# A recommender tower on one core: the end after the last interaction layer is computed in another order

## The chip, the cores and the metric

One Trainium2 chip, one of its cores. The metric is the device time of one launch in microseconds (us). The kernel before took 900.58 us, the median of 3 runs (899.3 to 905.62).

## The reference, cut to what matters

For each of 512 samples, 32 table rows of 32 numbers are looked up. Two interaction layers (CIN) follow, each of 128 maps, and three dense layers:

```
e   = gathered rows                              # (512, 32, 32): sample, field h, position d
c0  = relu(sum over h, m of  e[h] * e[m]  * filter_0[h, m, n])      # (512, 128, 32)
c1  = relu(sum over h, m of  e[h] * c0[m] * filter_1[h, m, n])      # (512, 128, 32)
z   = concat(sum over d of c0, sum over d of c1)                    # (512, 256)
h   = concat(z, dense_ctx)                                          # (512, 272), dense_ctx is (512, 16)
h   = maximum(h @ W_top1 + b_top1, 0)                               # (512, 512)
h   = maximum(h @ W_top2 + b_top2, 0)                               # (512, 256)
y   = h @ W_top3                                                    # (512, 1)
```

All of it is float32. The kernel calls the sum over d of c0 `h0`, and the sum over d of c1 `h1`.

## The kernel before, in words

**Tiles.** A tile is 4 samples by 32 positions, 128 rows. There are 128 tiles, in 32 groups of four; a group is 512 columns wide. `over_groups` (L91) writes groups 0, 1, 29, 30 and 31 out one by one and loops over those between. `u` is the tile in its group, 0 to 3.

**Products in two halves.** Most products split an operand into a rounded part in the format fp32r (`_hi`) and the remainder, whole minus rounded part (`_lo`). They compute hi*hi, hi*lo and lo*hi, three TensorE instructions of 512 columns (L637, L638, L643 for the second interaction layer). A product of two plain float32 tiles, such as L693, is one call that the trace shows as two MATMUL instructions.

**The second interaction layer** is nearly all of the time. Each tile has eight banks of 512 columns, `k` = 0 to 7. TensorE (PE) computes a bank in one of six PSUM buffers in turn (RING). ScalarE (ACT) takes banks 0, 1, 3, 5, 6 out with the scale by the embedding (L399, four instructions of 128 columns to a bank), and VectorE (DVE) takes banks 2, 4, 7 (L523). A bank can be written anew once the one six before it has been taken out. GpSimd (POOL) adds two quarters of a tile's products once banks 0 to 3 are out (`fold`, L330). DVE then sums the rest in two halves (`reduce`, L537), and takes the maximum with zero (`rectify`, L544), which signals `c1_ready`. PE sums over d by a product of 4 columns (`sum_h1`, L648), three tiles later.

**Orders.** Each engine runs its own instructions in the order in which they are written. DVE's order in a tile is: bank 2, second half of `reduce` of two tiles before, bank 4, `rectify` of two tiles before, first half of `reduce` of the tile before, bank 7. In the last group (31) no interaction of a further group is prepared, and there DVE also rounds the weights of the top layers (`round_top`, L565, L569) in tiles 1 and 2, and POOL computes their remainders (L358) after the folds of tiles 2 and 3.

**The end.** After the last bank, PE runs `sum_h1` of tile 1, then for each of four blocks `j` of 128 outputs the float32 products with h0 (L693) and with the 16 dense columns (L694), both in plain float32. It then runs `sum_h1` of tiles 2 and 3. ACT copies `h1` rounded out of PSUM in two pieces (L439: 504 columns early, the last 8 late), DVE forms its remainder (L602), and PE runs 12 products of 512 columns with h1 (L701, L702, L705). ACT then reads each block of the first dense layer twice, rounded and whole, both with the bias (L443, L444); DVE subtracts (L605). PE runs 24 products of the second dense layer (L710, L711, L714), ACT rectifies twice (L447), PE runs the last product (L720), ACT copies it (L449), and SP writes it out (L282).

**Queues.** SP issues all other transfers, among them seven for the top layers (L268 to L274) behind those of group 2. POOL issues the gathers.

## Time and profile before

| | |
|---|---|
| median of 3 runs | 900.58 us |
| profiled execution: time | 904.71 us |
| profiled execution: span of the core | 902.9 us |
| PE busy | 879.3 us, 97% |
| DVE busy | 780.5 us, 86% |
| ACT busy | 782.9 us, 87% |
| POOL busy | 750.6 us, 83% |
| granted clock, mean over the span | 0.989 |
| transfers in the first of 40 slices of the span | 179 GB/s |

Times in the rows further down are us from the start of the span. A busy time of PE counts matmuls whose ends are modelled, and neighbours overlap; the distance from start to start is what one costs. The granted clock is given as a share of full speed: 1.00 is 2.4 GHz and 0.50 is 1.2 GHz.

### The profile page before, as it was taken

Reading aid. Unit: us, or ns where it says so; the run is one execution under the profiler, and the core shown is the slowest. Engines: PE = TensorE matmul, PEld = TensorE weight load, DVE = VectorE, ACT = ScalarE, POOL = GpSimd, SP = SyncE. Lnnn points to the kernel's source line nnn. Section 1 sums busy time; section 2 is a strip of 40 time slices with the busy share of each in tenths; the row PEclk is TensorE's granted clock in tenths of the full one; section 3 lists DMA queues with packets and bytes.
Section 4 is the critical chain, followed back from the end, with each engine's and each line's share of the span. In section 5 each row is a group of like instructions: output and inputs, shape, how many; then the busy total and the mean of one; then the engine's idle time right before and its main releaser. Section 6 shows DMA issues by size and latency. Waiting matters only on the chain.

```text
span 902.9 us, 17442 instructions
## 1 busy us (share of the span) xinstructions
PE 879.3 (97%) x3758; PEld 689.7 (76%) x3758; DVE 780.5 (86%) x903; ACT 782.9 (87%) x2744; POOL 750.6 (83%) x542
## 2 busy tenths in 40 slices
PE   3899999999999999999999999999999999999988
PEld 2678877777887777788777778877777887777844
DVE  4588888999888899988889998888989888898991
ACT  2699899999989999999989999989999999999942
POOL 5599889898888989888898988889899898988430
PEclk9999999999999999999999999999999999999987
DMA  5432222221222222122222212222221122220000
GB/s 179 127 115 79 80 74 78 78 64 34 67 78 73 77 78 68 33 64 78 73 77 78 68 35 61 78 73 77 78 75 33 56 78 73 77 78 1 1 1 0
DMA packets 42810, 60.85 MB, mean 67 GB/s; under 512 B 6274, under 2 KB 17154, under 8 KB 42787
## 3 DMA queue, kind: packets, MB, share of 16 engines
q1 hardware_dynamic: 38690, 58.48, 21.1%
q0 software_dynamic: 4096, 2.11, 1.6%
q8 instruction: 9, 0.15, 0.1%
q14 instruction: 15, 0.11, 0.0%
HBM read 56.37 MB, written 4.20 MB: 67 GB/s over the span
## 4 chain that ended last, share of the span: by engine, by line
PE 95%; DMA 1%; ACT 1%; DVE 1%; issue 1%; POOL 0%; SPq 0%; DVEq 0%; ACTq 0%; POOLq 0%
PE ps_y L637 27%; PE ps_y L643 26%; PE ps_y L638 26%; PE ps_c L616 6%; PE ps_h L648 2%; PE ps_c L625 2%; PE ps_c L624 2%; PE ps_c L626 2%; PE ps_c L622 1%; ACT prod L399 1%; PE ps_y L694 1%; PE ps_y L693 1%; DMA second<-et_scratch 1%; DMA gat<-table,rows_now 0%; POOL gat L292 0%
## 5 line engine op out<-in xcount | busy, mean ns | idle before, releaser
L399 ACT ACTIVATE prod<-ps_y,es 128x128 f32<-128x128 f32 x2560 | 715.7, 434 | 72.7 <-PE ps_y L643 68.7
L537 DVE TENSOR_REDUCE csum<-prod 128x64 f32<-128x1536 f32 x256 | 447.3, 1748 | 10.4
L637 PE MATMUL ps_y<-w_hi,c_hi 128*128 128x512 f32 x1024 | 437.3, 427 | 2.1 <-ACT prod L399 1.3
L643 PE MATMUL ps_y<-w_hi,c_lo 128*128 128x512 f32 x1024 | 400.9, 392 | 0.0
L638 PE MATMUL ps_y<-w_lo,c_hi 128*128 128x512 f32 x1024 | 400.4, 391 | 0.0
L330 POOL TENSOR_TENSOR prod<-prod 128x1024 f32<-128x1024 f32 x128 | 308.3, 2408 | 55.6 <-ACT prod L399 48.8
L523 DVE TENSOR_TENSOR prod<-ps_y,es 128x512 f32<-128x512 f32 x384 | 256.8, 682 | 76.2 <-PE ps_y L643 72.8
L637 PEld LDWEIGHTS ps_y<-w_hi,c_hi 128*128 128x128 f32 x1024 | 192.8, 188 | 54.7 <-issue 18.2
L638 PEld LDWEIGHTS ps_y<-w_lo,c_hi 128*128 128x128 f32 x1024 | 192.9, 188 | 50.2 <-issue 14.9
L643 PEld LDWEIGHTS ps_y<-w_hi,c_lo 128*128 128x128 f32 x1024 | 192.1, 188 | 43.4
L321 POOL TENSOR_TENSOR z<-first,second 128x512 f32<-128x512 f32 x155 | 198.6, 1299 | 9.1 <-DMA second<-et_scratch 9.1
L292 POOL DMA_INDIRECT gat<-table,rows_now x128 | 124.8, 975 | 52.9 <-POOL rows_now L303 26.2
L311 POOL TENSOR_TENSOR z_lo<-z,z_hi 128x512 fp32r<-128x512 f32 x93 | 118.9, 1296 | 0.0
L616 PE MATMUL ps_c<-z,w_sum 128*128 128x512 f32 x128 | 65.3, 591 | 0.7 <-DVE z L492 0.7
L368 ACT ACTIVATE z_hi<-z 128x512 fp32r<-128x512 f32 x64 | 51.3, 801 | 12.0 <-DVE z L492 11.1
L648 PEld LDWEIGHTS ps_h<-ones_b,c 128*128 128x128 f32 x256 | 48.2, 190 | 13.0 <-issue 1.5
L544 DVE TENSOR_REDUCE c<-csum 128x128 f32<-128x256 f32 x128 | 52.1, 407 | 0.1
L648 PE MATMUL ps_h<-ones_b,c 128*128 128x4 f32 x256 | 36.3, 213 | 0.8 <-DVE c L544 0.8
L616 PEld LDWEIGHTS ps_c<-z,w_sum 128*128 128x128 f32 x128 | 23.9, 188 | 6.4 <-DVE z L492 1.5
L624 PE MATMUL ps_c<-z_hi,w_hi 128*128 128x512 f32 x64 | 25.8, 403 | 1.5 <-DVE z_lo L557 1.5
L625 PE MATMUL ps_c<-z_hi,w_lo 128*128 128x512 f32 x64 | 26.2, 409 | 0.0
L626 PE MATMUL ps_c<-z_lo,w_hi 128*128 128x512 f32 x64 | 26.0, 406 | 0.0
(65 smaller groups left out, 278.0 us busy)
## 6 DMA issues: line engine op xcount, KB each, us to landing
second<-et_scratch SPq DMA_DIRECT2D x160, 256.0 KB, 4.4
first<-et_scratch SPq DMA_DIRECT2D x32, 256.0 KB, 3.3
et_scratch<-gat SPq DMA_DIRECT2D x64, 64.0 KB
prod<-w SPq DMA_DIRECT2D x4, 512.0 KB, 7.1
gat<-table,rows_now POOLq DMA_INDIRECT x128, 2.4
wt_sb<-wt SPq DMA_DIRECT2D x2, 512.0 KB
prod<-w0a SPq DMA_DIRECT2D x1, 320.0 KB, 3.0
prod<-w0b SPq DMA_DIRECT2D x1, 320.0 KB, 3.3
```

What stands on the lines that cost most here:

```text
L292: pool.indirect_dma_start(out=gat[:, g.r, u * D:(u + 1) * D], out_offset=None, in_=table, in_offset=bass.IndirectOffsetOnAxis(ap=rows_now[ ...
L311: nc.gpsimd.tensor_tensor(z_lo[:, k, :], z[:, k, :], z_hi[:, k, :].bitcast(F32), ALU.subtract).then_inc(z_lo_ready, 1)
L321: nc.gpsimd.tensor_tensor(z[:, k, :], first[:, :], second[:, k, :], ALU.mult).then_inc(z_ready, 1)
L330: nc.gpsimd.tensor_tensor(high, high, low, ALU.add).then_inc(folded, 1)
L399: last = nc.scalar.activation(prod[:, buffer_of(g, u), h // 2, :, h % 2], ps_y[:, bank_of(g, u, k), j * N:(j + 1) * N], ACT.Copy, scale=es ...
L523: nc.vector.tensor_tensor(prod[:, buffer_of(g, u), pairs, :, :], ps_y[:, bank_of(g, u, k), :].rearrange("p (a n t) -> p a n t", n=N, t=2), ...
L537: nc.vector.tensor_reduce(csum[:, maps, 0], prod[:, buffer_of(g, u), FOLD // 2:F // 2, maps, :].rearrange("p a n t -> p n a t"), AX.XY, AL ...
L616: nc.tensor.matmul(ps_c[:, :], w0_sum[:, k, :], z[:, k, :].rearrange("p (b u d) -> p u b d", u=TG, b=BT), start=(k == 0), stop=False)
L637: nc.tensor.matmul(out, hi, w_hi, start=True, stop=False)
L638: nc.tensor.matmul(out, hi, w_lo, start=False, stop=False)
L643: nc.tensor.matmul(out, lo, w_hi, start=False, stop=True).then_inc(y_ready, 1)
L648: nc.tensor.matmul(ps_h1[:, bass.ds(g.times(TG * BT, u * BT), BT)], c1[:, u % 2, :], ones_b[:, :], start=True, stop=True).then_inc(h1_done, 1)
```

## The change

It concerns the last group and what comes after it.

- The dense columns are stacked with the bias. The host builds an operand of 81 rows: three copies of the 16 dense columns at rows 0, 32 and 64, and a row of ones behind the first and the third; for the weights the bias stands in these rows. On the chip both operands are rounded. In rows 32 to 47 of the values and rows 64 to 80 of the weights the remainder takes the place of the rounded part (`stack_rest`). One product then gives hi*hi, lo*hi and hi*lo, with the bias in it.
- h0 is split into `h0_hi` and `h0_lo`, and its part of the first layer is three fp32r products for each block in place of one in float32.
- The products with h1 are divided by columns: the first 504 (`early`) come before `sum_h1` of the last two tiles, the last 8 (`late`) behind it. ACT copies the early columns twice, and POOL forms the early remainder; DVE forms the late one.
- Ten products whose result nobody reads (KEEP_WARM) stand before `sum_h1` of the last two tiles.
- The roundings of the weights are on ACT (five `round_top`), and POOL has three remainders, of wt2, of both halves of wt1, and of h0.
- ACT reads each block of the first dense layer once. DVE takes the remainder from PSUM, as max(x, 0) minus the rounded part.
- SP issues six transfers for the top layers; the two for the dense columns have 81 rows in place of 16.

```diff
 B, F, D, N, DENSE = 512, 32, 32, 128, 16
 TOP1, TOP2 = 512, 256
+STACK = 64 + DENSE + 1
...
+        dense_x_sb = sb("dense_x_sb", [STACK, B])
+        dense_w_sb = sb("dense_w_sb", [STACK, TOP1])
+        dense_x_r = sb("dense_x_r", [STACK, B], F32R)
+        dense_w_r = sb("dense_w_r", [STACK, TOP1], F32R)
+        h0_hi = sb("h0_hi", [P, B], F32R)
+        h0_lo = sb("h0_lo", [P, B], F32R)
+        h1 = sb("h1", [P, B])
...
+        wt1_hi = sb("wt1_hi", [P, 2, TOP1], F32R)
+        wt1_lo = sb("wt1_lo", [P, 2, TOP1], F32R)
...
-        a1 = z[:, 0:4, :]
...
-        wt1_hi, wt1_lo = z_hi[:, 2, :], z_lo[:, 2, :]
...
+        early, late = slice(0, BT * (TILES - 2)), slice(BT * (TILES - 2), B)
...
-            sp.dma_start(wt1_d[:, :], wt1[2 * P:2 * P + DENSE, :]).then_inc(top_in, 16)
+            sp.dma_start(dense_w_sb[:, :], dense_w).then_inc(top_in, 16)
             sp.dma_start(wt2_sb[:, :, :], wt2.rearrange("(k p) n -> p k n", p=P)).then_inc(top_in, 16)
             sp.dma_start(wt3_sb[:, :], wt3).then_inc(top_in, 16)
-            sp.dma_start(bt1_sb[:, :], bt1).then_inc(top_in, 16)
             sp.dma_start(bt2_sb[:, :], bt2).then_inc(top_in, 16)
-            sp.dma_start(hd[:, :], dense_t).then_inc(top_in, 16)
+            sp.dma_start(dense_x_sb[:, :], dense_x).then_inc(top_in, 16)
...
-                    if number == GROUPS - 1 and u >= 2:
-                        low, whole, high = ((wt2_lo, wt2_sb[:, :, :], wt2_hi), (wt1_lo, wt1_sb[:, 1, :], wt1_hi))[u - 2]
-                        pool.wait_ge(top_hi_ready, u - 1)
-                        nc.gpsimd.tensor_tensor(low, whole, high.bitcast(F32), ALU.subtract).then_inc(top_lo_ready, 1)
+                    if number == GROUPS - 1:
+                        for n in ((0,), (1,), (2,), ())[u]:
+                            low, whole, high = remainders[n]
+                            pool.wait_ge(top_hi_ready, (1, 2, 5)[n])
+                            nc.gpsimd.tensor_tensor(low, whole, high.bitcast(F32), ALU.subtract).then_inc(top_lo_ready, 1)
+            remainders = ((wt2_lo, wt2_sb[:, :, :], wt2_hi), (wt1_lo[:, :, :], wt1_sb[:, :, :], wt1_hi[:, :, :]),
+                          (h0_lo[:, :], h0[:, :], h0_hi[:, :]))
             over_groups(pool, body)
+            pool.wait_ge(h1_ready, 1)
+            pool.wait_ge(h1_hi_ready, 1)
+            nc.gpsimd.tensor_tensor(h1_lo[:, early], h1[:, early], h1_hi[:, early].bitcast(F32),
+                                    ALU.subtract).then_inc(h1_lo_ready, 1)
...
+            def round_top(out, whole):
+                nc.scalar.activation(out, whole, ACT.Copy).then_inc(top_hi_ready, 1)
...
+                        if number == GROUPS - 1 and (u, k) == (0, 4):
+                            act.wait_ge(top_in, TOP_LOADS * 16)
+                            act.wait_ge(l0_done, GROUPS)
+                            round_top(wt2_hi, wt2_sb[:, :, :])
+                        if number == GROUPS - 1 and (u, k) == (1, 1):
+                            round_top(wt1_hi[:, :, :], wt1_sb[:, :, :])
+                        if number == GROUPS - 1 and (u, k) == (1, 5):
+                            round_top(dense_x_r[:, :], dense_x_sb[:, :])
+                        if number == GROUPS - 1 and (u, k) == (2, 1):
+                            round_top(dense_w_r[:, :], dense_w_sb[:, :])
+                        if number == GROUPS - 1 and (u, k) == (2, 4):
+                            act.wait_ge(h0_done, GROUPS)
+                            round_top(h0_hi[:, :], h0[:, :])
...
-            for tiles in (range(TILES - 2), range(TILES - 2, TILES)):
-                act.wait_ge(h1_done, tiles.stop)
-                cols = slice(BT * tiles.start, BT * tiles.stop)
-                nc.scalar.activation(h1_hi[:, cols], ps_h1[:, cols], ACT.Copy).then_inc(h1_hi_ready, 1)
-            act.wait_ge(top_in, 7 * 16)
+            act.wait_ge(h1_done, TILES - 2)
+            nc.scalar.activation(h1_hi[:, early], ps_h1[:, early], ACT.Copy).then_inc(h1_hi_ready, 1)
+            nc.scalar.activation(h1[:, early], ps_h1[:, early], ACT.Copy).then_inc(h1_ready, 1)
+            act.wait_ge(h1_done, TILES)
+            nc.scalar.activation(h1_hi[:, late], ps_h1[:, late], ACT.Copy).then_inc(h1_hi_ready, 1)
             for j in range(TOP1 // P):
                 act.wait_ge(mm_top, j + 1)
-                nc.scalar.activation(a1_hi[:, j, :], ps_a1[j], ACT.Relu, bias=bt1_sb[:, j:j + 1]).then_inc(a1_hi_ready, 1)
-                nc.scalar.activation(a1[:, j, :], ps_a1[j], ACT.Relu, bias=bt1_sb[:, j:j + 1]).then_inc(a1_ready, 1)
+                nc.scalar.activation(a1_hi[:, j, :], ps_a1[j], ACT.Relu).then_inc(a1_hi_ready, 1)
...
-            def round_top(out, whole):
-                dve.wait_ge(top_in, 7 * 16)
-                dve.wait_ge(l0_done, GROUPS)
-                nc.vector.tensor_copy(out, whole).then_inc(top_hi_ready, 1)
+            def stack_rest(rounded, whole, at, rows):
+                dve.wait_ge(top_hi_ready, at)
+                nc.vector.tensor_tensor(rounded[rows, :], whole[rows, :], rounded[rows, :].bitcast(F32),
+                                        ALU.subtract).then_inc(stacked_rest, 1)
...
-                        if number == GROUPS - 1 and (u, k) == (1, 3):
-                            round_top(wt2_hi, wt2_sb[:, :, :])
                         if number == GROUPS - 1 and (u, k) == (2, 3):
-                            round_top(wt1_hi, wt1_sb[:, 1, :])
+                            stack_rest(dense_x_r, dense_x_sb, 3, slice(32, 32 + DENSE))
+                        if number == GROUPS - 1 and (u, k) == (3, 1):
+                            stack_rest(dense_w_r, dense_w_sb, 4, slice(64, STACK))
...
             dve.wait_ge(h1_hi_ready, 2)
-            nc.vector.tensor_tensor(h1_lo, ps_h1[:, :], h1_hi.bitcast(F32), ALU.subtract).then_inc(h1_lo_ready, 1)
+            nc.vector.tensor_tensor(h1_lo[:, late], ps_h1[:, late], h1_hi[:, late].bitcast(F32),
+                                    ALU.subtract).then_inc(last_h1_lo, 1)
             for j in range(TOP1 // P):
-                dve.wait_ge(a1_ready, j + 1)
-                nc.vector.tensor_tensor(a1_lo[:, j, :], a1[:, j, :], a1_hi[:, j, :].bitcast(F32),
-                                        ALU.subtract).then_inc(a1_lo_ready, 1)
+                dve.wait_ge(a1_hi_ready, j + 1)
+                nc.vector.scalar_tensor_tensor(out=a1_lo[:, j, :], in0=ps_a1[j], scalar=0.0, in1=a1_hi[:, j, :].bitcast(F32),
+                                               op0=ALU.max, op1=ALU.subtract).then_inc(a1_lo_ready, 1)
...
-            pe.wait_ge(top_in, 7 * 16)
-            pe.wait_ge(h0_done, GROUPS)
+            pe.wait_ge(top_lo_ready, 3)
+            pe.wait_ge(stacked_rest, 2)
             for j in range(TOP1 // P):
                 pe.wait_ge(act_scaled, signals(ACT_BANKS, LAST, TG - 1, NK - RING + j))
                 pe.wait_ge(dve_scaled, signals(DVE_BANKS, LAST, TG - 1, NK - RING + j))
                 cols = slice(j * P, (j + 1) * P)
-                nc.tensor.matmul(ps_a1[j], wt1_sb[:, 0, cols], h0[:, :], start=True, stop=False)
-                nc.tensor.matmul(ps_a1[j], wt1_d[:, cols], hd[:, :], start=False, stop=False)
+                nc.tensor.matmul(ps_a1[j], dense_w_r[:, cols], dense_x_r[:, :], start=True, stop=False)
+                nc.tensor.matmul(ps_a1[j], wt1_hi[:, 0, cols], h0_hi[:, :], start=False, stop=False)
+                nc.tensor.matmul(ps_a1[j], wt1_lo[:, 0, cols], h0_hi[:, :], start=False, stop=False)
+                nc.tensor.matmul(ps_a1[j], wt1_hi[:, 0, cols], h0_lo[:, :], start=False, stop=False)
+            def add_h1(j, columns, weights, values, stop):
+                return nc.tensor.matmul(ps_a1[j][:, columns], weights[:, 1, j * P:(j + 1) * P], values[:, columns],
+                                        start=False, stop=stop)
             pe.wait_ge(h1_hi_ready, 1)
+            for j in range(TOP1 // P):
+                add_h1(j, early, wt1_hi, h1_hi, False)
+                add_h1(j, early, wt1_lo, h1_hi, False)
+            pe.wait_ge(h1_lo_ready, 1)
+            for j in range(TOP1 // P):
+                add_h1(j, early, wt1_hi, h1_lo, False)
+            pe.wait_ge(act_scaled, signals(ACT_BANKS, LAST, TG - 1, 6))
+            for n in range(KEEP_WARM):
+                nc.tensor.matmul(ps_a2[0], wt1_hi[:, 0, 0:P], wt1_hi[:, 1, :], start=True, stop=True)
             sum_h1(LAST, TG - 2)
             sum_h1(LAST, TG - 1)
-            pe.wait_ge(top_lo_ready, 2)
+            pe.wait_ge(dve_scaled, signals(DVE_BANKS, LAST, TG - 1, NK - 1))
             pe.wait_ge(h1_hi_ready, 2)
             for j in range(TOP1 // P):
-                nc.tensor.matmul(ps_a1[j], wt1_hi[:, j * P:(j + 1) * P], h1_hi, start=False, stop=False)
-                nc.tensor.matmul(ps_a1[j], wt1_lo[:, j * P:(j + 1) * P], h1_hi, start=False, stop=False)
-            pe.wait_ge(h1_lo_ready, 1)
+                add_h1(j, late, wt1_hi, h1_hi, False)
+                add_h1(j, late, wt1_lo, h1_hi, False)
+            pe.wait_ge(last_h1_lo, 1)
             for j in range(TOP1 // P):
-                nc.tensor.matmul(ps_a1[j], wt1_hi[:, j * P:(j + 1) * P], h1_lo, start=False, stop=True).then_inc(mm_top, 1)
+                add_h1(j, late, wt1_hi, h1_lo, True).then_inc(mm_top, 1)
...
+def stacked(rows, last):
+    out = np.zeros((STACK, rows.shape[1]), np.float32)
+    for at in (0, 32, 64):
+        out[at:at + DENSE] = rows
+    for at in (0, 64):
+        out[at + DENSE] = last
+    return out
...
-        "dense_t": np.ascontiguousarray(x["dense_ctx"].T),
+        "dense_x": stacked(x["dense_ctx"].T, np.ones((1, B), np.float32)),
+        "dense_w": stacked(x["W_top1"][2 * P:], x["b_top1"][None, :]),
```

## Rows read from the trace of the kernel before

**Rows 1.** The timeline of PE at the end: start, us, engine, line, operation, [idle before]

```profile
871.45 0.39 PE L648 MATMUL ps_h<-ones_b,c 128*128 128x4 f32 x2 [0.77 <-DVE c L544]
871.69 1.10 PE L693 MATMUL ps_y<-h,wt_sb 128*128 128x512 f32 x2
...
885.69 1.01 PE L648 MATMUL ps_h<-ones_b,c 128*128 128x4 f32 x4
887.07 0.77 PE L701 MATMUL ps_y<-z_hi 128*128 128x512 f32 x1 [0.36 <-ACT z_hi L439]
...
897.63 0.62 PE L714 MATMUL ps_y<-w_lo,z_hi 128*128 128x512 f32 x2
```

**Rows 2.** The chain that ended last, in order of time: start, us, what

```profile
888.26 0.43 PE ps_y L701
...
891.28 0.69 ACT w_hi L443
...
895.93 0.23 PE ps_y L710
...
898.06 0.70 ACT second L447
```

**Rows 3.** The timeline of DVE in the last group and behind it

```profile
856.26 1.70 DVE L569 CAST z_hi<-wt_sb 128x1024 fp32r<-128x1024 f32 x1
857.88 0.68 DVE L523 TENSOR_TENSOR prod<-ps_y,es 128x512 f32<-128x512 f32 x1
...
863.54 1.26 DVE L569 CAST z_hi<-wt_sb 128x512 fp32r<-128x512 f32 x1
864.73 0.68 DVE L523 TENSOR_TENSOR prod<-ps_y,es 128x512 f32<-128x512 f32 x1
...
867.53 1.28 DVE L523 TENSOR_TENSOR prod<-ps_y,es 128x512 f32<-128x512 f32 x2
...
870.99 0.41 DVE L544 TENSOR_REDUCE c<-csum 128x128 f32<-128x256 f32 x1
...
879.57 0.42 DVE L544 TENSOR_REDUCE c<-csum 128x128 f32<-128x256 f32 x1
```

**Rows 4.** The timeline of ACT in the last group and behind it

```profile
846.41 8.51 ACT L399 ACTIVATE prod<-ps_y,es 128x128 f32<-128x128 f32 x32
...
871.87 0.59 ACT L439 ACTIVATE z_hi<-ps_h 128x504 fp32r<-128x504 f32 x1 [0.36 <-PE ps_h L648]
886.75 0.18 ACT L439 ACTIVATE z_hi<-ps_h 128x8 fp32r<-128x8 f32 x1 [14.28 <-PE ps_h L648]
```

**Rows 5.** The timeline of POOL in the last group

```profile
862.11 2.41 POOL L330 TENSOR_TENSOR prod<-prod 128x1024 f32<-128x1024 f32 x1 [4.70 <-DVE prod L523]
864.48 2.58 POOL L358 TENSOR_TENSOR z_lo<-wt_sb,z_hi 128x1024 fp32r<-128x1024 f32 x1
```

**Rows 6.** Groups of instructions by shape: busy us in total, mean ns of one

```profile
L406 ACT ACTIVATE w_hi<-prod 128x512 fp32r<-128x512 f32 x8 | 4.6, 621 | 7.4 <-DMA prod<-w 7.4
...
L476 DVE CAST w_hi<-w_sum 128x640 fp32r<-128x640 f32 x1 | 0.5, 507 | 0.0
```

**Rows 7.** The timeline of PE near the start

```profile
24.50 1.12 PE L616 MATMUL ps_c<-z,w_sum 128*128 128x512 f32 x2 [0.65 <-DVE z L492]
27.15 0.59 PE L624 MATMUL ps_c<-z_hi,w_hi 128*128 128x512 f32 x1 [1.52 <-DVE z_lo L557]
```

**Rows 8.** Busy time in stretches of PE, PEld, DVE, ACT, POOL; then granted clock, DMA

```profile
28.00:30.00 2.00, 2.00 (x6) 1.30 (x4) 0.29 (x1) 0.00 (x0) 0.00 (x0) 0.50 0.47 127
...
877.00:880.00 3.00, 3.00 (x4) 0.82 (x4) 2.96 (x3) 0.00 (x0) 0.00 (x0) 0.50 0.02 5
...
891.00:892.00 1.00, 0.89 (x4) 0.37 (x2) 0.00 (x0) 0.72 (x2) 0.00 (x0) 1.00 0.00 0
```

**Rows 9.** The timeline of SP's queue while it issues the top layers' transfers

```profile
50.54 0.46 SPq L274 DMA_DIRECT2D hd<-dense_t  x1
58.40 1.25 SPq L249 DMA_DIRECT2D et_scratch<-gat  x2
```

More of the change, by code:

```diff
@@ L32 @@
 TOP1, TOP2 = 512, 256
+STACK = 64 + DENSE + 1
+TOP_LOADS = 6
+KEEP_WARM = 10
 P = 128
@@ L103, with tower @@
 LAST = Group((GROUPS - 1) // SLOTS, (GROUPS - 1) % SLOTS)
-def tower(nc, ids, bounds, copy_of, table, dense_t, w0a, w0b, w1, wt1, bt1, wt2, bt2, wt3, y):
+def tower(nc, ids, bounds, copy_of, table, dense_x, dense_w, w0a, w0b, w1, wt1, wt2, bt2, wt3, y):
     ctx = ExitStack()
@@ L144, in tower @@
         h0 = sb("h0", [P, B])
-        hd = sb("hd", [DENSE, B])
+        dense_x_sb = sb("dense_x_sb", [STACK, B])
[5 more added lines that the diff above has]
+        h1 = sb("h1", [P, B])
         wt1_sb = sb("wt1_sb", [P, 2, TOP1])
-        wt1_d = sb("wt1_d", [DENSE, TOP1])
-        bt1_sb = sb("bt1_sb", [P, TOP1 // P])
+        wt1_hi = sb("wt1_hi", [P, 2, TOP1], F32R)
+        wt1_lo = sb("wt1_lo", [P, 2, TOP1], F32R)
         wt2_sb = sb("wt2_sb", [P, TOP1 // P, TOP2])
@@ L204, in tower @@
         h1_hi_ready = sem("h1_hi_ready")
+        h1_ready = sem("h1_ready")
+        stacked_rest = sem("stacked_rest")
         h1_lo_ready = sem("h1_lo_ready")
+        last_h1_lo = sem("last_h1_lo")
         top_hi_ready = sem("top_hi_ready")
@@ L208, in tower @@
         a1_hi_ready = sem("a1_hi_ready")
-        a1_ready = sem("a1_ready")
         a1_lo_ready = sem("a1_lo_ready")
@@ L776 @@
         "wt1": x["W_top1"],
-        "bt1": np.ascontiguousarray(x["b_top1"].reshape(TOP1 // P, P).T),
         "wt2": x["W_top2"],
```

## The prediction

> **What bounds the kernel now.** I read the engine table first: PE is busy 97% of the span, so what counts is where PE's order stretches. The change touches only the end, so I followed the chain of waits there. After the last bank, PE waits for DVE's `rectify` of tile 1 and starts `sum_h1` at 871.45. The float32 products with h0 and the dense columns run from 871.69 to 885.69, 14.0 us [rows 1]. During them the granted clock is at 1.2 GHz, 0.50 [rows 8]. The reader is to see what else these 14 us cover: DVE's last `rectify` ends at 879.99 [rows 3], so 5.7 us of them stand behind everything else. Then come `sum_h1` twice, ACT's copy of 8 columns, and twelve products of 512 columns at 0.43 us each [rows 1, 2]. ACT reads the first block at 891.28, and PE is back at 2.4 GHz [rows 2, 8]. From there a product costs 0.23 us, and ACT's first read of the second layer's result is at 898.06 [rows 2].
>
> In the last group DVE is the bound: its timeline shows no idle time from 856.26 to 879.99, and its two roundings stand in that line. The first takes from 856.26 to 857.88, 1.62 us of it, and the second from 863.54 to 864.73, 1.19 us [rows 3].
>
> **The change part by part.** Times are of the profiled execution (904.71 us, span 902.9), which lies 4.1 us above the median of 900.58. I work out the saving there and take it from the median.
>
> *DVE in the last group.* Removed: 1.62 + 1.19 = 2.81 us. Added: two `stack_rest` of 512 columns. Two `scale` of that width take 1.28 us together, start to start 0.60 [rows 3], so 1.20. Net 1.61 earlier. Beyond that lies a wait that the trace of before shows for the rounding it loses. A rounding of 640 columns alone took 0.51 us [rows 6]. The one of 512 columns, started at 863.54 while POOL ran a fold (862.11 + 2.41 = 864.52), ended only at 864.80, 0.28 after the fold [rows 3, 5]. So DVE waited for POOL, and then went ahead, although POOL's next instruction stood ready at 864.48. The new `stack_rest` read two SBUF tiles and may wait in the same way. No row of before has such an instruction beside POOL: its cost is between 0.60 and 0.60 plus one POOL instruction.
>
> *ACT in the last group* gets five roundings. 512 columns take 0.62 [rows 6]; 1024 columns lie between 0.62 and 1.24, and I take 1.1, near the double. Together 2 x 1.1 + 3 x 0.62 = 4.1 us. A bank costs 4 x 0.266 = 1.06 us (8.51 for 32) from 846.41 [rows 4]. ACT's 20 banks then end at 846.41 + 21.3 + 4.1 = 871.8, against 869.33 + 2.18 = 871.5 in the timeline of before: there it idles, and the new work fills the gaps. PE waits a little for banks. The last bank needs ACT's (3, 1), the 17th, at 846.41 + 18.1 + 4.1 = 868.6, and ends about 0.9 later, 869.5.
>
> *Where POOL stands.* ACT's eighth bank ends at 846.41 + 8.5 + 2.2 = 857.1. The fold of tile 1 follows (2.41), then the remainder of wt1 (2.58 [rows 5]), to 862.1. The first `stack_rest` arrives at 863.54 - 1.62 = 861.9 and waits 0.2. ACT's 13th bank ends at 846.41 + 13.8 + 2.2 + 1.2 = 863.6, the fold of tile 2 at 866.0, the remainder of h0 (half of 2.58) at 867.3. The second `stack_rest` arrives at 867.53 - 2.81 + 0.60 + 0.2 + 0.60 = 866.1. This is a tie. I take it that DVE gets in with no wait, as in the row of the rounding that went ahead, and keep 1.3 us as the other end.
>
> *PE's tail* starts behind `rectify` of tile 1: 871.40 - 2.81 + 1.20 + 0.2 = 870.0, later than its last bank. `sum_h1` 0.24 (871.45 to 871.69) [rows 1]. Then 16 + 8 + 4 + 10 = 38 products at 0.23 [rows 2], 8.74 us, to 879.0. Their operands are ready: bank 5 leaves ACT one bank before its end, at 870.7. ACT's two copies of 504 columns (0.59 each [rows 4]) end at 873.0, and POOL's remainder (1.3) at 874.3; PE wants it at 870.3 + 24 x 0.23 = 875.8. If that cover went, PE would wait for the difference. DVE's last `rectify` ends at 879.99 - 1.41 = 878.6. PE is 0.4 later, so of the 2.3 us of the ten dummy products only this 0.4 is on the path.
>
> *The narrow part.* Two `sum_h1`: four instructions took 1.01 at 1.2 GHz [rows 1]; half of it, 0.5. From the last of them over ACT's 8 columns to PE's next product: 887.07 - 886.72 = 0.35 (885.69 + 1.01, then the 0.18 of ACT [rows 4] and the signals). Then 8 narrow products and the first of the last four. The nearest row is 1.01 us for four of 4 columns at 1.2 GHz, so 0.25 each, 0.12 at 2.4 GHz; the ends are 0 and 0.25. Nine are 1.1, and 0.2 for the last one to drain. DVE's remainder of 8 columns is hidden under the eight: even 512 columns take 0.68 [rows 3]. Signal to ACT 0.1. Sum: 879.0 + 0.5 + 0.35 + 1.3 + 0.1 = 881.2, against 891.28: **10.1 us earlier**.
>
> *The second dense layer.* Before: 898.06 - 891.28 = 6.78. After: ACT 0.69, signal 0.05, 24 products at 0.23 = 5.5, drain and signal 0.2: 6.45. The remainder no longer waits for ACT's second read: it is there at 0.69 + 0.05 + 0.68 = 1.4, and PE wants it at 0.74 + 0.92. **0.3 us**. What follows stays.
>
> *Transfers.* One fewer, two larger by 65 rows of 2 KB, 0.27 MB. They stand behind group 2's, and SP issues nothing from 51.0 to 58.40 [rows 9]. Nothing, or 1.5 us if that cover is gone (0.27 MB at the 179 GB/s of the page's first slice, in the table above).
>
> Sum: 10.1 + 0.3 = 10.4. 900.58 - 10.4 = **890.2 us** (894.3 in a profile like this one).
>
> **The rivals.**
>
> 1. *POOL holds the second `stack_rest`* until its remainder of h0 is done. For: the tie above and the waiting rounding. Against: that one went ahead. Both of PE's gates, `rectify` of tiles 1 and 3, move by 1.3: 891.5 us. The Trainium skill, "SBUF — State Buffer", section "Who interferes with whom", says that a DVE instruction with two SBUF inputs contends with a GpSimd instruction that reads SBUF, and that issue order decides which one is blocked. By that rule the time is that of this rival, or of the forecast if DVE is first; the trace agrees as far as the rounding's 1.26 us goes, which has one input.
>
> 2. *The clock drops behind the dummies.* From 879.0 to 881.9 PE has only narrow work, 2.9 us. Near the start PE had 1.12 us of work in the 2.65 us from 24.50 to 27.15 [rows 7], and the clock was then at 0.50 from 28 to 30 [rows 8]. It comes back: in the tail of before the first 512-column fp32r product starts at 887.07 and the clock is at 1.00 from 891 [rows 1, 8]. For these 3.9 us at most a product costs 0.43 in place of 0.23 [rows 2]: 9 products where 17 would go, 1.8 us: 892.0 us. Against: the 38 products before it are dense.
>
> 3. *ACT becomes the bound.* Its last group is 21.3 us of banks and 4.1 of roundings for 22 us of PE. If the roundings cost twice as much, PE's last bank comes 4.1 later, less 0.5 of slack: 893.8 us.
>
> 4. *Slower: the clock stays at 1.2 GHz through the whole tail*, as it did from 877 to 880 in before [rows 8]. 62 products x 0.20 = 12.4 and 16 narrow ones x 0.12 = 1.9 make 14.3: 904.5 us. It decides from about 50 of the 62 at the low level. Against: the float32 products go, and twice in the trace a stream of 512-column fp32r products brought the clock back, before 891 within 4 us of 887.07 [rows 1, 8].
>
> **How the numbers follow.** Forecast 0.42, with its own range of 888.7 (narrow products at 0) to 891.8 (at 0.25 each); POOL's hold 0.20; the clock spell 0.25; ACT 0.09; slower 0.04. The range 888.2 to 894.0 takes in the first three and most of the fourth. 1% is 9.0 us, 891.6: about what a measurement can tell, as the three runs span 6.3 us. Faster by over 1% holds nine tenths of the forecast, half of the first rival and a third of the second: 0.56. Slower 0.04, the rest 0.40. The gain and the bound lie close together, so this is nearly a coin.
>
> **What would show it.** In the profile after: no idle time of DVE in the last group, and PE's tail at 870.0 (tie lost: 871.3, with a `stack_rest` of over 1 us); the 38 products at 0.23 with clock 1.00; DVE's last `rectify` before the last dummy; 2.2 us from there to ACT's first read; 24 products in 5.5 us, or 7 and a clock of 0.50. I am wrong if PE's last bank comes after 870, if a narrow product costs over 0.25, or if the loop over the groups changes its length.

## The result and the profile after

The changed kernel takes 895.81 us, the median of 22 runs (893.09 to 899.15), against 900.56 us for the kernel before (22 runs, 896.11 to 906.83). The ratio is 0.9942, with a 95% interval of 0.9926 to 0.9959: 0.6% faster; 0.0058 of 900 us is 5.2 us. The forecast was 890.2 us, with a range of 888.2 to 894.0. The sign was right; the gain was half of the forecast.

The profiled execution of the changed kernel took 895.66 us with a span of 893.8. The one of before took 904.71 with 902.9. So the two profiles lie 9.1 us apart while the medians lie 4.8 apart, and the question is where this difference comes from.

The timeline of PE in the changed kernel answers to [rows 1]:

```profile
870.05 0.39 PE L681 MATMUL ps_h<-ones_b,c 128*128 128x4 f32 x2 [1.70 <-DVE c L576]
870.29 0.48 PE L726 MATMUL ps_y<-dense_x_r,dense_w_r 81*128 81x512 f32 x1
...
876.85 2.44 PE L744 MATMUL ps_y<-wt_hi 128*128 128x512 f32 x10
879.12 0.50 PE L681 MATMUL ps_h<-ones_b,c 128*128 128x4 f32 x4
879.98 0.24 PE L732 MATMUL ps_y<-z_hi,wt_hi 128*128 128x8 f32 x1 [0.36 <-ACT z_hi L473]
880.09 0.25 PE L732 MATMUL ps_y<-z_hi,wt_lo 128*128 128x8 f32 x1
...
883.88 0.63 PE L760 MATMUL ps_y<-w_hi,z_lo 128*128 128x512 f32 x1
884.30 0.63 PE L759 MATMUL ps_y<-w_hi,z_hi 128*128 128x512 f32 x1
```

The tail starts at 870.05, as forecast, and the 38 products end at 879.12. A narrow product costs 0.11 from start to start. In the second dense layer products are 0.42 apart in the middle (883.88 to 884.30), as long as in the tail of before at 1.2 GHz (0.43, [rows 2]). The busy times in stretches show the clock there, in the column before the last two:

```profile
882.00:883.00 1.00, 1.00 (x5) 0.82 (x5) 1.00 (x3) 1.00 (x3) 0.00 (x0) 1.00 0.00 0
883.00:884.00 1.00, 1.00 (x5) 0.77 (x4) 1.00 (x3) 0.22 (x1) 0.00 (x0) 0.56 0.00 0
884.00:886.00 2.00, 2.00 (x6) 1.53 (x5) 0.27 (x1) 0.00 (x0) 0.00 (x0) 0.50 0.00 0
886.00:887.00 1.00, 1.00 (x5) 0.81 (x4) 0.00 (x0) 0.00 (x0) 0.00 (x0) 0.73 0.00 0
```

DVE in the changed kernel, answering to [rows 3]:

```profile
861.69 0.68 DVE L600 TENSOR_TENSOR dense_x_r<-dense_x_sb,dense_x_r 16x512 fp32r<-16x512 f32 x1
...
865.22 0.68 DVE L555 TENSOR_TENSOR prod<-ps_y,es 128x512 f32<-128x512 f32 x1
865.94 0.76 DVE L600 TENSOR_TENSOR dense_w_r<-dense_w_sb,dense_w_r 17x512 fp32r<-17x512 f32 x1
...
869.59 0.41 DVE L576 TENSOR_REDUCE c<-csum 128x128 f32<-128x256 f32 x1
...
875.08 3.41 DVE L569 TENSOR_REDUCE csum<-prod 128x64 f32<-128x1536 f32 x2 [0.49 <-DVE c L576]
878.53 0.42 DVE L576 TENSOR_REDUCE c<-csum 128x128 f32<-128x256 f32 x1
```

And ACT, answering to [rows 4]: the roundings, the 8 columns, its reads of both dense layers.

```profile
849.06 1.22 ACT L408 ACTIVATE z_hi<-wt_sb 128x1024 fp32r<-128x1024 f32 x1
...
854.01 1.35 ACT L408 ACTIVATE wt_hi<-wt_sb 128x1024 fp32r<-128x1024 f32 x1
...
879.66 0.18 ACT L473 ACTIVATE z_hi<-ps_h 128x8 fp32r<-128x8 f32 x1 [8.11 <-PE ps_h L681]
881.16 2.07 ACT L476 ACTIVATE w_hi<-ps_y 128x512 fp32r<-128x512 f32 x4 [1.32 <-PE ps_y L732]
889.01 1.27 ACT L479 ACTIVATE second<-ps_y,bt_sb 128x512 f32<-128x512 f32 x2 [5.79 <-PE ps_y L763]
```

Every execution also comes with PE's mean granted clock. These are all executions of before that ran beside the experiments (96), and of the changed kernel (22 and the 12 of the last experiment), grouped by it:

| mean clock | before: executions | median us | changed: executions | median us |
|---|---|---|---|---|
| 1.000 | 9 | 896.3 | 7 | 893.6 |
| 0.998 | 16 | 897.5 | 17 | 895.7 |
| 0.996 | 19 | 898.3 | 2 | 896.1 |
| 0.994 | 11 | 899.9 | 7 | 898.2 |
| 0.992 | 14 | 901.6 | 1 | 900.3 |
| 0.991 | 14 | 903.7 | 0 | |
| 0.989 | 11 | 904.7 | 0 | |
| 0.987 | 2 | 906.1 | 0 | |

The clock orders the medians, on both chips that the 96 ran on. It is not all of the spread: executions of one kernel at the same clock still differ by up to 2.5 us (893.92 to 896.41 for the changed kernel at 0.998), and in profiled executions with the clock at 1.00 from the start to the last group DVE reaches the same instruction of that group anywhere from 845.43 (e6) to 847.94 (e4). The profiled execution of before had 0.989, near the bottom; the middle one of the 96 has 0.994. At full clock the kernels are 2.7 us apart.

The profile of before itself shows what a float32 call costs at either level, and when the clock fell:

```profile
872.73 1.12 PE L694 MATMUL ps_y<-hd,wt_d 16*128 16x512 f32 x2
873.78 1.97 PE L693 MATMUL ps_y<-h,wt_sb 128*128 128x512 f32 x2
875.68 2.07 PE L694 MATMUL ps_y<-hd,wt_d 16*128 16x512 f32 x2
```

```profile
873.00:874.00 1.00, 1.00 (x3) 0.24 (x3) 1.00 (x3) 0.00 (x0) 0.00 (x0) 0.96 0.00 0
874.00:875.00 1.00, 1.00 (x2) 0.18 (x1) 1.00 (x1) 0.00 (x0) 0.00 (x0) 0.50 0.00 0
```

The first two calls run at full clock, 1.04 and 1.05 us from start to start (871.69, 872.73, 873.78); the later ones take about 2.0. So the prediction's reading that the clock is at 0.50 during all 14.0 us isn't right: it fell at 873.9, in the third call, and was back at 891.0, 17 us later. Eight calls at 1.05 are 8.4 us.

Theory A, which the experiments test, is this: in an execution at full clock the float32 products are nearly free, since they would end about 8.4 us behind 871.69, at 880.1, and DVE's last rectify ends no earlier than 879.99 [rows 3]. The 9 us of the profiles are mostly time at 1.2 GHz that most executions of before have only in part. The rival B: the float32 products cost every execution what the profile shows, and the changed kernel loses 4 us elsewhere.

### The profile page after: what moved, and what is told of

It reads as the page before. It is cut to its first block, busy times and chain, and to the rows that moved or that the text cites. A ratio compares the mean times of both kernels' runs of the same rounds, so it can differ in the third digit from the quotient of the medians.

```text
span 893.8 us, 17487 instructions
## 1 busy us (share of the span) xinstructions
PE 869.2 (97%) x3780; PEld 690.6 (77%) x3780; DVE 778.4 (87%) x903; ACT 784.1 (88%) x2746; POOL 753.9 (84%) x544
## 4 chain that ended last, share of the span: by engine, by line
PE 91%; DVE 2%; issue 2%; POOL 2%; DMA 2%; SPq 0%; ACT 0%; DVEq 0%; POOLq 0%
PE ps_y L670 26%; PE ps_y L676 25%; PE ps_y L671 25%; PE ps_c L649 6%; PE ps_c L657 2%; PE ps_c L658 2%; PE ps_c L659 2%; PE ps_h L681 2%; PE ps_c L655 1%; DVE csum L569 1%; DVE prod L555 1%; POOL gat L302 1%; POOL prod L340 1%; DMA second<-et_scratch 1%; DMA gat<-table,rows_now 0%
## 5 line engine op out<-in xcount | busy, mean ns | idle before, releaser
L331 POOL TENSOR_TENSOR z<-first,second 128x512 f32<-128x512 f32 x155 | 198.9, 1302 | 10.4 <-DMA second<-et_scratch 10.4
```

What stands on the lines that cost most here:

```text
L331: nc.gpsimd.tensor_tensor(z[:, k, :], first[:, :], second[:, k, :], ALU.mult).then_inc(z_ready, 1)
```

## The experiments

**e1: the float32 products back, no dummies.** Against the changed kernel:

```diff
-KEEP_WARM = 10
+KEEP_WARM = 0
-                nc.tensor.matmul(ps_a1[j], dense_w_r[:, cols], dense_x_r[:, :], start=True, stop=False)
-                ... wt1_hi x h0_hi, wt1_lo x h0_hi, wt1_hi x h0_lo
+                nc.tensor.matmul(ps_a1[j], wt1_sb[:, 0, cols], h0[:, :], start=True, stop=False)
+                nc.tensor.matmul(ps_a1[j], dense_w_sb[0:DENSE + 1, cols], dense_x_sb[0:DENSE + 1, :], start=False, stop=False)
```

> The changed kernel with the h0 and dense products of the first layer in float32 again (the dense one with the bias row, 17 rows) and without the ten dummy products; all else as changed. Theory A (the profiled execution of before was a long one: its products ran at 1.2 GHz for 17 us at the end, which most executions do not; at 2.4 GHz the float32 products take 8.3 us and lie almost wholly under DVE's last reductions): at full clock these products end at 870.3 + 8.3, the twelve early ones add 2.8, so PE comes to the last two sums 2.3 us later than in the changed kernel. Fastest execution 2 to 3 us above the changed kernel's fastest (893.1), so about 895.5; median 898 to 900, with mean clocks between 0.990 and 1.00 that order the times. Theory B (the float32 products always cost what the profile shows, and the changed kernel loses some 4 us elsewhere): every execution 7 us or more above the changed kernel, 902 to 904, no execution near 896.

Measured: 898.04 us, the fastest 895.44; ratio to before 1.0022 (0.9982 to 1.0062). Seven of 12 executions lie at 898.04 or below, with clocks of 0.998 and 1.00; the others are between 905.9 and 909.0, with clocks of 0.985 to 0.989. The timeline of PE in its profiled execution, which kept the clock there:

```profile
869.61 1.10 PE L726 MATMUL ps_y<-h,wt_sb 128*128 128x512 f32 x2
...
878.02 0.50 PE L730 MATMUL ps_y<-z_hi,wt_hi 128*128 128x504 f32 x1
...
880.87 0.50 PE L681 MATMUL ps_h<-ones_b,c 128*128 128x4 f32 x4
```

The eight calls take 8.4 us here, against 14.0 in [rows 1], the same work. B is refuted: seven executions are as good as A says. The other five cost some 10 us more, at clocks that are lower by 0.01; where in the kernel their clock fell is not seen.

**e5: before, with 8 products more.** Against the kernel before:

```diff
                 nc.tensor.matmul(ps_a1[j], wt1_sb[:, 0, cols], h0[:, :], start=True, stop=False)
+                nc.tensor.matmul(ps_c[:, :], w0_hi[:, 0, :], w0_hi[:, 0:BANK // N, :].rearrange("p k n -> p (k n)"), start=True, stop=True)
                 nc.tensor.matmul(ps_a1[j], wt1_d[:, cols], hd[:, :], start=False, stop=False)
+                ... the same product again (written as a loop in the kernel that ran)
```

> The kernel before with one dummy product of 512 columns in fp32r behind each of its 8 float32 calls in the tail, nothing else. Work is only added: 8 x 0.23 = 1.9 us. Theory A (the float32 products, though PE is busy, let the clock fall, and that fall is what the long executions of before consist of): the dummies keep the clock at 2.4 GHz; the fastest execution is 1.5 to 1.9 us slower than before's fastest (895.2), so 897, but the long ones of 901 to 906 go, and the median is at or below before's 899. Theory C (the rival now: the clock falls because of the wait ahead of the tail or by chance, whatever the products are): every execution 1.9 us or more slower, the median 901, and executions above 904 remain.

Measured: 898.98 us, the fastest 896.53; ratio 0.9997 (0.9967 to 1.0027), with before at 900.45 beside it. One of 12 executions is above 901 (908.11, clock 0.987); of the 35 of before beside it 17 are, all with clocks of 0.992 or less, and of all 96 it is 41. Its timeline of PE and two stretches:

```profile
872.23 1.12 PE L697 MATMUL ps_y<-hd,wt_d 16*128 16x512 f32 x2
873.28 0.50 PE L698 MATMUL ps_c<-w_hi 128*128 128x512 f32 x1
...
881.34 0.50 PE L648 MATMUL ps_h<-ones_b,c 128*128 128x4 f32 x4
...
883.81 0.63 PE L707 MATMUL ps_y<-z_hi,z_lo 128*128 128x512 f32 x1
```

```profile
878.00:882.00 4.00, 3.84 (x13) 1.67 (x11) 1.23 (x2) 0.12 (x1) 0.00 (x0) 1.00 0.00 0
...
883.00:886.00 3.00, 3.00 (x9) 2.32 (x8) 0.00 (x0) 0.19 (x1) 0.00 (x0) 0.50 0.00 0
```

The float32 calls stay at 1.05 (872.23 to 873.28) throughout, and the clock falls only later. This profile alone proves little, since in e1's the clock held with no product added; the evidence is the count of long executions. PE was busy with float32 products in before too, and with an fp32r product behind each call long executions became rare. Theory C, the chance or the wait ahead, expected 901 and times above 904 as before. The added work isn't free: at clock 1.000 the four executions of e5 have a median of 898.3, 2 us above before's 896.3. In the median this is made up by the long executions that are missing.

All runs together say the same. Before, e1 and e6 have the eight float32 calls in a row: of their executions, 52 of 120 have a clock of 0.992 or less, and 50 take over 901 us. Of all others, e5 among them (127 executions), 4 have such a clock, and one takes over 901 us.

**e6: before, with the roundings on ACT.** One part of the change alone:

```diff
-                        if number == GROUPS - 1 and (u, k) == (1, 3):
-                            round_top(wt2_hi, wt2_sb[:, :, :])
-                        ... and (2, 3) for wt1_hi, both on DVE
+                        if number == GROUPS - 1 and (u, k) == (0, 4):
+                            nc.scalar.activation(wt2_hi, wt2_sb[:, :, :], ACT.Copy).then_inc(top_hi_ready, 1)
+                        ... and (1, 1) for wt1_hi, both on ACT, with the waits of the old ones
```

> The kernel before with one part of the change: the two roundings of the top weights are on ACT, in banks (0, 4) and (1, 1) of the last group, in place of DVE. DVE loses 2.8 us from the line that sets the start of PE's tail and its last rectify. Theory A (at full clock the float32 products lie under DVE's reductions, so the gate is DVE in fast executions and PE in long ones, and both start 2.8 us earlier): 2.5 to 2.8 us faster at each clock, fastest 892.5, median 896 to 896.5, with the same spread of clocks as before. That would be as much as the whole change gives in the median. If the float32 products were the cost in every execution, it would give the same 2.8 and the whole change 5 more; so what counts is its fastest execution against the changed kernel's fastest, 893.1: at or below it by theory A, 3 us or more above it by theory B.

Measured: 897.46 us, the fastest 894.18; ratio 0.9978 (0.9946 to 1.0010). No execution had clock 1.000. At 0.998 its three have a median of 894.6, against 897.5 for before: 2.9 less. Its fastest is 1.1 above the changed kernel's, between what A (at or below it) and B (3 or more above it) gave it. PE, and DVE's last rectify:

```profile
866.95 1.11 PE L689 MATMUL ps_y<-h,wt_sb 128*128 128x512 f32 x2
...
870.09 1.12 PE L690 MATMUL ps_y<-hd,wt_d 16*128 16x512 f32 x2
871.14 2.07 PE L689 MATMUL ps_y<-h,wt_sb 128*128 128x512 f32 x2
...
879.15 1.02 PE L644 MATMUL ps_h<-ones_b,c 128*128 128x4 f32 x4
```

```profile
874.83 0.42 DVE L550 TENSOR_REDUCE c<-csum 128x128 f32<-128x256 f32 x1
```

Half of the float32 calls run at full clock and half at the low one, in one execution. DVE is done at 875.25; eight calls at full clock would have ended at 866.95 + 8.4 = 875.35, and they end at 879.15.

This run also shows what the changed kernel gives away on DVE. Counted from the same instruction at the last group's start (845.43 here, 847.38 in before, 847.02 in the changed kernel), DVE's last rectify ends after 32.61 us in before, 31.93 in the changed kernel and 29.82 in e6. Moving the roundings alone gains 2.8 us there; the changed kernel keeps 0.7 of it, since its two `stack_rest` and the idle time ahead of the last reductions stand in the same line. At clock 0.998 e6 has 894.6 (three executions) and the changed kernel 895.7. The changed kernel with these two remainders on another engine was not tried.

**e7: the split and the stacked columns alone.** The changed kernel without dummies, with 12 whole h1 products behind the last sum, and with ACT reading the first layer twice (`a1`, `a1_ready` and L605 as before).

> The changed kernel with the column division, the dummy products and the remainder from PSUM undone: 12 whole h1 products behind the last sum, none of the ten dummies, ACT reads the first layer twice. What is left of the change is the split h0, the stacked dense columns and the roundings on ACT. Theory A: at full clock 1.2 us over the changed kernel for the 9 wide products and 0.3 for the second read, 894.6 to 895 in the fastest; PE idles from about 874 to 879, so the clock is low in the h1 products in most executions: median 898 to 899.5, clocks of 0.996 and below. Without the clock's part (theory B) it is 1.5 us over the changed kernel throughout.

Measured: 897.60 us, the fastest 895.77; ratio 0.9973 (0.9952 to 0.9994). One of 12 executions has a clock above 0.996. The fastest lies 1 us above what A gave, and no execution kept the clock, so the full-clock time was not seen. The median lies below A's 898 to 899.5 and near what was expected without the clock, 1.5 above the changed kernel: 897.3. So the time alone doesn't speak for A here; the low clocks do, as A had it. In the profiled execution the clock is low from 876.8, while PE waits for DVE, to 883.6.

**e2: no dummies.** `KEEP_WARM = 0` in the changed kernel.

> The changed kernel without its ten dummy products. Theory A: PE waits idle for DVE's last rectify from about 876.9 to 879, so the clock falls more often behind it: fastest execution the same as the changed kernel's (893.1, or 0.2 less), median 1 to 3 us above it, mean clock mostly 0.994 and below. Theory B (the clock has no part in the missing gain): within 0.3 us of the changed kernel, the same clocks.

Measured: 896.24 us, the fastest 895.04; ratio 0.9957 (0.9932 to 0.9982). All 12 executions have 0.996 or 0.994, against 10 of 34 at 0.996 or below with the dummies. In the profiled execution PE idles 1.88 us for DVE's last rectify, and from 879.6 to 886.5 the clock is low; narrow products are then 0.21 apart. So the dummies do keep the clock up, but A had the sizes wrong: the fastest loses 1.9 us where A had it unchanged, and the median 0.4 where A had 1 to 3.

**e3: h1 not divided.** The changed kernel with 12 h1 products of 512 columns behind the last sum, and 22 dummies ahead of it.

> The changed kernel with the h1 product not divided: all twelve products have 512 columns and come behind the last sum, DVE forms the whole remainder, and 22 dummy products stand ahead in place of the 12 early ones and 10 dummies. Theory A: 9 products of 512 columns at 0.23 where 9 narrow ones at 0.11 stood, and ACT's read starts about 1.2 us later; at full clock 1.2 us over the changed kernel, and since PE is dense there the spell of low clock in the second layer is rarer, so the median is only 0 to 1 us above the changed kernel's. Theory B: 1.2 to 1.5 us above it in the median as in the fastest.

Measured: 896.51 us, the fastest 894.17; ratio 0.9967 (0.9941 to 0.9993). The fastest is 1.1 above the changed kernel's and the median 0.7, as A had it. Its profiled execution shows another place at which the clock falls, behind PE's wait ahead of the tail:

```profile
872.38 0.39 PE L676 MATMUL ps_h<-ones_b,c 128*128 128x4 f32 x2 [1.63 <-ACT prod L415]
...
873.36 0.63 PE L723 MATMUL ps_y<-h_hi,wt_lo 128*128 128x512 f32 x1
873.78 0.63 PE L724 MATMUL ps_y<-h_lo,wt_hi 128*128 128x512 f32 x1
...
876.82 0.39 PE L724 MATMUL ps_y<-h_lo,wt_hi 128*128 128x512 f32 x1
```

The clock is low there from 873.0 to 876.4, and near the start too, from 26.4 to 33.3. Behind the last sums it is at 1.00, and this gives the price of the undivided products at full clock:

```profile
883.57 0.18 ACT L468 ACTIVATE z_hi<-ps_h 128x8 fp32r<-128x8 f32 x1 [10.17 <-PE ps_h L676]
886.27 2.07 ACT L471 ACTIVATE w_hi<-ps_y 128x512 fp32r<-128x512 f32 x4 [2.52 <-PE ps_y L727]
```

From ACT's copy of the 8 columns to its first read of the first layer it is 2.70 us here and 881.16 - 879.66 = 1.50 in the changed kernel: 1.2 more.

**e4: dummies in the narrow part.** One more behind the last sum, two ahead of the second layer.

> The changed kernel with three more dummy products of 512 columns: one while PE waits for ACT's copy of the last 8 columns, two while it waits for ACT's first read of the first layer. Both holes were idle (0.36 and 0.35 us plus the narrow products' drain). Theory A: less low clock in the second layer; fastest execution 0 to 0.3 us above the changed kernel's, median 0.5 to 2 us below it. Theory B: 0 to 0.3 us above it in both.

Measured: 896.00 us, the fastest 893.22; ratio 0.9956 (0.9931 to 0.9981). The median did not fall, where A had it 0.5 to 2 lower. A's expectation failed: the narrow part is not the only place.

**e8: dummies at the start.** Eight products ahead of `layer0`'s third step.

> The changed kernel with 8 dummy products at the start, in the 2.1 us in which PE waits for DVE's first z_lo ahead of layer0's third step; the end is as changed. Theory A (some of the executions at 0.998 and less have their low stretch there, as the profile of before has it at 27 to 31): median 0.3 to 1 us below the changed kernel's, more executions at clock 1.00, fastest unchanged. If that low stretch costs nothing (the engines behind PE are not waiting there): no difference in time, though the clock rises.

Measured: 895.80 us, the fastest 894.14; ratio 0.9950 (0.9926 to 0.9973). No difference to the changed kernel in the median, where A had 0.3 to 1 less; two of 12 executions have clock 1.000. In the profiled execution the clock is at 1.00 at the start and low from 881.2 to 884.6, behind the narrow products, as in the changed kernel's.

**e9: reordered.** The changed kernel with the fillings of e4 and e8, 16 dummies, and the sum of tile 1 behind the first 8 products of h0:

```diff
-            sum_h1(LAST, TG - 3)
...
                 nc.tensor.matmul(ps_a1[j], wt1_hi[:, 0, cols], h0_lo[:, :], start=False, stop=False)
+                if j == 1:
+                    sum_h1(LAST, TG - 3)
```

> The changed kernel reordered against low clock: the sum of tile 1 comes behind the first 8 of the 16 products of h0, so PE does not idle 1.7 us for DVE ahead of the tail; 16 dummies in place of 10; one and two dummies in the two holes of the narrow part; 8 dummies at the start. Theory A (the clock is lost in four places: the start, the wait ahead of the tail, the wait for the last rectify, the narrow part): all four are filled, most executions at 0.998 or 1.00, fastest as the changed kernel's (893.1) or 0.3 more, median 893.7 to 894.5. If one of the places filled is not where the clock is lost, the median stays at 895 to 896.

Measured: 893.51 us (892.61 to 895.12); ratio 0.9920 (0.9894 to 0.9946). Nine of 11 executions have clock 1.000, two 0.998, as A had it. PE no longer idles ahead of the tail:

```profile
868.67 0.39 PE L734 MATMUL ps_y<-h_lo,wt_hi 128*128 128x512 f32 x1
868.89 0.33 PE L683 MATMUL ps_h<-ones_b,c 128*128 128x4 f32 x2
869.08 0.48 PE L731 MATMUL ps_y<-dense_x_r,dense_w_r 81*128 81x512 f32 x1
```

**e10: POOL folds twice.** e9 with 12 dummies, and for the last tile:

```diff
+            nc.gpsimd.tensor_tensor(third, third, fourth, ALU.add).then_inc(folded, 1)
-... prod[:, buffer_of(g, u), FOLD // 2:F // 2, maps, :] ...
+... prod[:, buffer_of(g, u), FOLD // 2:F // 2 - more_folded * FOLD // 2, maps, :] ...
```

> e9_reordered with 12 dummies, and GpSimd adds two more quarters of the last tile's products, so that DVE's two last reductions read 1024 in place of 1536 numbers to a row. Each is 0.5 us shorter; DVE must wait for GpSimd until about 875.3, 0.2 later than it starts now. If DVE's last rectify is what ends last ahead of the narrow part (theory A), 0.7 to 0.9 us faster than e9_reordered at each clock: fastest 892.3, median 893 to 893.7. If PE's own products bound the tail, no difference.

Measured: 892.88 us (891.87 to 893.77); ratio 0.9917 (0.9888 to 0.9946). Nine of 10 executions have clock 1.000. DVE's last reductions and rectify, in e9 and then in e10:

```profile
872.96 0.42 DVE L578 TENSOR_REDUCE c<-csum 128x128 f32<-128x256 f32 x1
873.87 3.41 DVE L571 TENSOR_REDUCE csum<-prod 128x64 f32<-128x1536 f32 x2 [0.49 <-DVE c L578]
877.31 0.42 DVE L578 TENSOR_REDUCE c<-csum 128x128 f32<-128x256 f32 x1
```

```profile
873.05 0.42 DVE L582 TENSOR_REDUCE c<-csum 128x128 f32<-128x256 f32 x1
874.18 2.35 DVE L575 TENSOR_REDUCE csum<-prod 128x64 f32<-128x1024 f32 x2 [0.71 <-POOL prod L382]
876.56 0.42 DVE L582 TENSOR_REDUCE c<-csum 128x128 f32<-128x256 f32 x1
```

From one rectify to the next it is 4.35 in e9 and 3.51 in e10, 0.8 less; the median gives 0.6 of it, the fastest 0.7. So at full clock DVE's last rectify is what PE's end waits for.

**e11: the changed kernel again**, beside e9 and e10.

> The changed kernel itself once more, on the same chip as the two above. Fastest 893.1, median 895.8 to 896.2, executions at 0.994 and near 898 among them; the kernel before beside it spreads from 895 to 906 in the order of its mean clock.

Measured: 895.30 us (893.32 to 900.28); ratio 0.9938 (0.9908 to 0.9967), before at 901.90 beside it. So e9 and e10 beat both kernels on one chip, by 1.8 and 2.4 us over the changed one. At clock 1.000 e9 (893.4) and the changed kernel here (893.7, four executions) are only 0.3 apart: the gain of e9 is mostly that its executions keep the clock. For the other experiments the changed kernel did not run beside them, only before did; differences of 1 us to its 893.09 or 895.81 are within the spread of the executions.

## Why the prediction was wrong

The working inside the profile held, nearly step by step. The tail starts at 870.05 (870.0 forecast), the last sums at 879.12 (879.0), ACT's first read at 881.16 (881.2). DVE's last rectify ends at 878.95, 0.3 late, because of 0.49 idle ahead of its last reductions that before doesn't have. (The same instruction of DVE at the last group's start is at 847.38 in before and 847.02 here, so counted from there each of these is 0.4 later than forecast: the two `stack_rest` took 0.71 and 0.90 from start to start with their waits, not 0.60. That the times of the tail agree to 0.1 is in part luck, as the group began 0.4 earlier.) ACT's roundings of 1024 columns are shown with 1.22 and 1.35, but ACT's next instruction starts 0.95 and 0.96 after them (849.06 to 850.01, 854.01 to 854.97), so they cost less than my 1.1, and PE's last bank was done by 868.4, not 869.5. The tie on DVE, rival 1: the second `stack_rest` came at 865.22 + 0.60 = 865.82, started at 865.94 and took 0.76 beside POOL's remainder of h0 in its last 0.2 us. It cost 0.2, not 1.3. The Trainium skill, "SBUF — State Buffer", section "Who interferes with whom", says that a DVE instruction with two SBUF inputs contends with a GpSimd instruction that reads SBUF. The late start and the longer run (0.76 against 0.68 for the first `stack_rest`, which had no POOL instruction beside it) agree with this, but POOL had only 0.2 us left, so the larger price was not put to the test.

Rival 2 occurred in the profiled execution: the clock is low from 883.1 to 886.5, and ACT's read of the second layer comes 889.01 - 881.16 = 7.85 after the first against my 6.45, 1.4 more. In e11's profile, at clock 1.00, it is 6.31. The profile time is 895.66 against 894.3 forecast, 1.4 off. I had this at a chance of 0.25; 27 of 34 executions are below 1.000, though not necessarily at this place. A slip that changes nothing: the forecast's own range of 888.7 to 891.8 moves twelve narrow products, while the sum has nine on the path (889.1 to 891.4).

**The step that failed** stands at the head of the costing: "I work out the saving there and take it from the median". The profiled execution of before stood 4.1 us above its median, and I treated that as an offset common to both kernels. It is not: those 4.1 us, and more, are the low clock in the tail, which is just what the change removes. The median execution of before has it only in part, and the one at full clock hardly at all. Of the 10.4 us that I took off, about 8 are owed to the low clock: the float32 calls took 14.0 us against 8.4 at full clock (e1), 5.6 more, and the twelve h1 products 0.43 each against 0.23, 2.4 more. The medians are 4.8 us apart, the profiles 9.1. Against the executions at full clock (896.3, known only from the experiments) the gain is 2.7: DVE's last rectify is 0.7 earlier, counted from the last group; dividing the h1 products gives 1.2 (e3); and the second layer takes 6.31 (e11) against 6.78, 0.5 less. That is 2.4; the rest, 0.3, is not assigned and lies within the spread.

The fact was in the text: the runs of before spread over 6.3 us, and 17 us at 1.2 GHz in the tail were seen. What I didn't ask is whether the two belong together.

Shown by e1, e5 and e9: most of the spread is the clock, and with other products between the float32 calls, or in place of them, nearly all long executions are gone. Whether the format of the added products matters, or only that something else stands between the calls, was not tried. Open: why one execution of a kernel keeps the clock and the next does not; only profiled executions have a trace, so the places of the low clock in the others are not seen. e4, e8 and e9 together say that filling one place is not enough, but not which of the places in e9 decides: the reordered sum and the longer row of dummies were not tried apart.

## What to carry to other kernels

Where runs of one kernel spread by more than the effect that is forecast, look first at what orders them, here the mean granted clock, and say where in that order the profiled execution stands. A saving that is read in a stretch at low clock is owed only to the executions that have it. And the work in a tail is to be compared with the engine that it waits for at full clock: 8.4 us of float32 products beside 8.5 us of DVE (871.45 to 879.99) were about level with it, and became the bound when the clock fell.

## What was not expected of the hardware

- PE's clock can fall while PE is busy without a gap with float32 products: in before at 873.9, in the third call, and in e6 at 871.2, at the start of the fifth. It doesn't always (e1's profile has 1.00 in all eight). With one 512-column fp32r product behind each call, 1 of 12 executions had a clock of 0.992 or less, against 17 of 35 beside it.
- Adding 1.9 us of PE work to the kernel before made its median no longer (ratio 0.9997), although it costs 2 us at full clock.
- 8-column products follow each other at 0.11 us at 2.4 GHz (879.98 to 880.09) and at 0.21 at 1.2 GHz (e2), so 64 times fewer columns are only half as long.
